# One-hots times the cutoff: made and stored in the one-head attention, loaded by the filter

## The chip, the cores and the metric

The kernel is one program on one core of a Trainium2 chip. A core has five engines, each with its own queue of instructions: TensorE (PE), VectorE (DVE), ScalarE (ACT), GpSimd (POOL), and SyncE (SP), which issues DMA transfers. Semaphores tie them together. The metric is the device time of one execution in microseconds (us), less is better.

## The reference

A graph network on 3125 nodes and 50000 edges: four layers, each with a residual and a layer norm. All of it is float32. Two parts matter here. The third attention of the second layer has one head of 128 channels; the filter of the third layer multiplies each edge's message by a filter and a cutoff, and sums the messages by destination:

```python
def _rgat(x, src, dst, etype, W, Q, K, b, heads, out_ch, n):      # third call: heads 1, out_ch 128
    ...
    alpha = _segment_softmax(alpha, dst, n)
    msg = (out_j.reshape(-1, heads, out_ch) * alpha[..., None]).reshape(-1, heads * out_ch)
    return jax.ops.segment_sum(msg, dst, num_segments=n) + b

h1 = h @ aw_W + aw_b                                              # the filter: _L2_gnn_ref
C = 0.5 * (jnp.cos(edge_weight * (PI / CUTOFF)) + 1.0)
Wf = ssp(ssp(edge_attr @ m1_W + m1_b) @ m2_W + m2_b)
Wf = Wf * C[:, None]
msg = h1[src] * Wf
agg = jax.ops.segment_sum(msg, dst, num_segments=n_nodes)
```

## The kernel before

The edges are sorted by destination and dealt into KS = 432 steps of P = 125 edges, each step belonging to one tile of 125 destination nodes. Both parts sum a step's messages by one product on PE: a one-hot matrix of 125 edges by 125 places in the tile (`sel`), times the 125 rows of messages. The one-hot is made by DVE: `iota` compared with `dloc`, the place of each edge's destination, for HF = 4 steps in one operation of 125x500. `cut` holds the cutoff of each edge.

**attention** runs three times: twice with four heads (H == 4) and last with one (H == 1, phase "sum3", the narrow attention). It goes by blocks of T = 12 steps, NS = 36 blocks, each in PARTS = 3 parts of four steps. POOL gathers the source rows of each step by an indirect DMA into `gx`, which holds three blocks; it waits only for the products that read the buffer three blocks back (`summed`). DVE scores the block after next as soon as its twelve gathers have landed (`score`), computes the softmax weights of the next block, and between these makes the one-hots of each part (`pick`, which counts `parted`) and adds PE's products to `agg` (`add_part`). ACT scales the gathered rows by the weights; PE does the products. SP loads one mask per block when `mask_used` says that a buffer is free. At the start of a block DVE's queue reads six numbers from memory into registers (`part_tiles`): which tile each part begins in, and whether a part spans two tiles, in which case its four steps are added one by one.

**filter_sum** goes by turns of four steps, 108 turns, in a loop of two (`q` is 0 or 1). POOL gathers the rows of `h2` into `gx`; SP loads the edges' attributes (`ea`). PE computes the hidden layer (`hidden`, L2390), the filter (`filters`, L2400) and the sums by destination (L2417). ACT computes the logarithms of softplus. The order is written out by hand, and several turns are in flight. In turn n DVE copies the cutoffs (`cl`, L2484), makes the one-hots (`sel`, L2485), finishes the filter `f2` once ACT's logarithm of turn n is there (L2489), multiplies filter, cutoff and gathered rows, one operation a step (`ms`, L2493), counts `ms_made` for PE and `used` for POOL, reads the tile numbers (`node_tiles`), finishes the hidden layer of turn n + 3 (`make_h1`, L2460), takes PE's filter product of turn n + 2 (`make_f2`, L2464), and adds PE's sums of turn n to `agg` (four operations, L2503).

Between the two lies nodes_mix, which works on nodes, not on edges.

## Time and profile before

| what | us |
|---|---|
| device time, median of 3 runs | 6739.39 (6736.36 to 6741.33) |
| profiled execution, device time | 6756.12 |
| its span | 6754.3 |
| granted TensorE clock over the span | 0.769 |
| one-head attention, gathers of POOL first to last issue | 3782.3 to 4440.3 |
| filter, loop of 108 turns | about 4694 to 5837 |

The profiled execution is 16.7 us above the median of the others, and 1.8 us of it lie outside the span. Times within the trace are us from the start of the span. "idle before <-releaser" is how long an engine stood still before an instruction and what ended it; "issue" is time in which its queue did work of its own (registers, branches, loads of numbers) and waited for nothing that the profile shows. DVEq and SPq are the queues of these engines.

### The profile page before, as it was taken

The numbers are of one execution on the slowest core, as the hardware profiler recorded it, in microseconds if no ns is written. First come the engines' busy times: TensorE is split into PE (matmuls) and PEld (weight loads), VectorE is DVE, ScalarE is ACT, GpSimd is POOL, SyncE is SP. The second block draws the span as 40 slices with busy tenths as digits, with TensorE's granted clock in tenths as the row PEclk, the third lists the DMA queues.
The fourth block names the chain that finished last, engine by engine and source line by source line (L and its number), as shares of the span: only waits on it lengthen the run. The fifth ranks groups of instructions, "written<-read, shape, count | busy, mean of one in ns | idle before, by whom it ended". The sixth has DMA issues, their size and how long they took to land. (4 is left out here: it accounts for less than half of the span.)

```text
span 6754.3 us, 80950 instructions
## 1 busy us (share of the span) xinstructions
PE 4441.0 (66%) x17924; PEld 3187.3 (47%) x17925; DVE 3214.4 (48%) x7726; ACT 2012.5 (30%) x4713; POOL 3593.5 (53%) x2941
## 2 busy tenths in 40 slices
PE   5699620885766778577677444467777777765553
PEld 5588610543555554455557333344545555443332
DVE  6566556213544522444443233343777777523334
ACT  0122200002655511455550122212555555410000
POOL 0244310467766647776647778721444444228885
PEclk9999855887887889787776555556999999876555
DMA  0000012225655523665532222222222222223333
GB/s 7 24 11 11 8 33 65 68 65 126 170 149 140 140 66 73 157 162 146 145 100 53 44 45 46 45 60 59 58 58 59 58 58 58 59 79 84 84 84 73
DMA packets 487821, 511.66 MB, mean 76 GB/s; under 512 B 307562, under 2 KB 372575, under 8 KB 487289
## 3 DMA queue, kind: packets, MB, share of 16 engines
q0 software_dynamic: 359872, 381.65, 23.6%
q1 hardware_dynamic: 127670, 127.35, 6.8%
q14 instruction: 233, 1.91, 0.1%
q8 instruction: 46, 0.75, 0.0%
HBM read 440.64 MB, written 65.22 MB: 75 GB/s over the span
## 5 line engine op out<-in xcount | busy, mean ns | idle before, releaser
L1198 POOL DMA_INDIRECT sum_gx_sb<-scratch_xw,keep_k_row_step_sb x1296 | 1599.8, 1234 | 564.1 <-issue 361.9
L1295 PE MATMUL sum_a_ps<-sum_gx_sb,sum_sel_sb 125*125 125x258 f32 (+1 forms) x4320 | 1241.6, 452 | 557.7 <-ACT sum_gx_sb L1231 234.9
L1295 PEld LDWEIGHTS sum_a_ps<-sum_gx_sb,sum_sel_sb 125*125 125x125 f32 x4320 | 955.9, 247 | 757.8 <-issue 563.2
L1231 ACT ACTIVATE sum_gx_sb<-sum_gx_sb,sum_wt_sb 125x129 f32<-125x129 f32 x3312 | 985.1, 398 | 492.5 <-DVE sum_wt_sb L1423 446.7
L2354 POOL DMA_INDIRECT filter_gx_sb<-scratch_h,keep_k_src_step_sb x432 | 520.6, 1205 | 678.0 <-DVEq L2495 531.7
L2782 POOL DMA_INDIRECT source_gx_sb<-scratch_h,source_grouped_sb x432 | 537.0, 1243 | 156.0 <-issue 118.9
L2794 PE MATMUL source_s_ps<-source_gx_sb,source_sel_sb 125*125 125x257 f32 x864 | 378.9, 615 | 313.6 <-DMA source_gx_sb<-scratch_h,source_grouped_sb 311.5
L1107 POOL DMA_INDIRECT scratch_grouped<-keep_k_value_sb,keep_k_place_sb x400 | 477.9, 1195 | 123.5 <-issue 123.5
L2400 PE MATMUL filter_ps<-filter_m_sb,filter_h_sb 128*125 128x256 f32 x1760 | 439.5, 406 | 39.9 <-DVE filter_f_sb L2464 39.9
L2794 PEld LDWEIGHTS source_s_ps<-source_gx_sb,source_sel_sb 125*125 125x125 f32 x864 | 252.5, 306 | 440.0 <-issue 196.3
L2400 PEld LDWEIGHTS filter_ps<-filter_m_sb,filter_h_sb 128*125 128x125 f32 x1760 | 343.9, 201 | 186.0 <-issue 132.7
L2417 PE MATMUL filter_ps<-filter_ms_sb,filter_sel_sb 125*125 125x256 f32 x864 | 243.2, 430 | 211.7 <-DVEq L2494 211.7
L2819 DVE TENSOR_TENSOR keep_agg_sb<-source_s_ps,keep_agg_sb 125x257 f32 x432 | 184.4, 427 | 395.4 <-PE source_s_ps L2794 384.3
L1443 DVE TENSOR_TENSOR keep_agg_sb<-sum_a_ps,keep_agg_sb 125x516 f32 (+1 forms) x360 | 202.3, 562 | 262.4 <-PE sum_a_ps L1295 143.0
L532 POOL TENSOR_TENSOR turn_lm_sb<-turn_lt_sb,turn_masks_sb 128x512 f32<-128x512 f32 x23 | 29.3, 1273 | 537.5 <-DVE turn_lt_sb L466 537.5
L1590 PE MATMUL attend_x_ps<-attend_w_sb,attend_ht_sb 128*125 128x512 f32 (+1 forms) x800 | 283.4, 528 | 37.3 <-ACT attend_ht_sb L2060 31.3
L2417 PEld LDWEIGHTS filter_ps<-filter_ms_sb,filter_sel_sb 125*125 125x125 f32 x864 | 170.2, 206 | 275.6 <-DVEq L2494 250.5
L2390 PE MATMUL filter_ps<-filter_ea_sb,filter_m_sb 51*128 51x500 f32 x444 | 239.8, 664 | 24.5 <-DMA filter_ea_sb<-in_ea_t 24.5
L2425 ACT ACTIVATE filter_lg_sb<-filter_f_sb 125x1024 f32<-125x1024 f32 x109 | 115.4, 1059 | 468.9 <-DVE filter_f_sb L2464 274.3
L2460 DVE SCALAR_TENSOR_TENSOR filter_h_sb<-filter_ps,filter_lg_sb 128x1000 f32<-128x1000 f32 x111 | 133.2, 1200 | 241.4 <-issue 202.2
L1430 DVE TENSOR_TENSOR sum_sel_sb<-sum_iota_sb,keep_k_dloc_sb 125x500 f32<-125x500 f32 x324 | 219.9, 679 | 50.7 <-issue 32.5
L2431 ACT ACTIVATE filter_lg_sb<-filter_lg_sb,filter_half_sb 128x1000 f32<-128x1000 f32 x220 | 238.8, 1132 | 7.6
(504 smaller groups left out, 7082.6 us busy)
## 6 DMA issues: line engine op xcount, KB each, us to landing
sum_gx_sb<-scratch_xw,keep_k_row_step_sb POOLq DMA_INDIRECT x1296
scratch_xw<-gate_xsb_sb SPq DMA_DIRECT2D x50, 253.9 KB
scratch_xw<-attend_xsb_sb SPq DMA_DIRECT2D x50, 253.9 KB
filter_ea_sb<-in_ea_t SPq DMA_DIRECT2D x444, 24.4 KB
filter_gx_sb<-scratch_h,keep_k_src_step_sb POOLq DMA_INDIRECT x432
source_gx_sb<-scratch_h,source_grouped_sb POOLq DMA_INDIRECT x432
sum_mk_sb<-scratch_masks SPq DMA_DIRECT2D x72, 93.9 KB
scratch_grouped<-keep_k_value_sb,keep_k_place_sb POOLq DMA_INDIRECT x400
```

The source lines that it names most:

```text
L1107: nc.gpsimd.indirect_dma_start(out=dr["grouped"], out_offset=bass.IndirectOffsetOnAxis(ap=keep["place"][:, t:t + 1], axis=0), in_=keep["va ...
L1198: nc.gpsimd.indirect_dma_start(out=gx[:, q, j, :], out_offset=None, in_=table, in_offset=bass.IndirectOffsetOnAxis(ap=keep["row_step"][:, ...
L1231: last = nc.scalar.activation(here, here, ACT.Copy, scale=wt[q][:, h, j:j + 1])
L1295: last = mm(psa[b][0:P, half, 0:BF], sel[:, 0, p, j, :], gx[:, q, at, half * BF:(half + 1) * BF], **flags)
L1590: mm(pr["psx"][r][0:P, 0:pr["width"]], x, pr["w"][:, b, r, :], start=(n == 0), stop=(n == len(blocks) - 1))
L2354: nc.gpsimd.indirect_dma_start(out=gx[:, q, j, :], out_offset=None, in_=dr["h2"], in_offset=bass.IndirectOffsetOnAxis(ap=keep["src_step"][ ...
L2390: last = mm(ps1[q][:, o, 0:C4], m1[0:51, 128 * o:128 * o + 128], ea[0:51, q].rearrange("p j e -> p (j e)"), start=True, stop=True)
L2400: last = mm(ps2[0:P, j, :], h1[q][:, b, j * P:j * P + P], m2[:, b, :], start=(b == 0), stop=(b == 1))
L2417: last = mm(ps3[0:P, j, :], sel[:, j, :], ms[:, j, :], start=True, stop=True)
L2431: nc.scalar.activation(lg[:], lg[:], ACT.Ln, scale=0.5, bias=half[0:lg.shape[0], :]).then_inc(made, 1)
L2782: nc.gpsimd.indirect_dma_start(out=gx[:, h % RING, j, :], out_offset=None, in_=dr["h3"], in_offset=bass.IndirectOffsetOnAxis(ap=grouped[:, ...
L2794: nc.tensor.matmul(pss[q % 2][0:P, j, 0:W], sel[:, q % 2, j, :], gx[:, q, j, :], start=True, stop=True).then_inc(summed, 1)
```

## The change

The one-hots of a step, times the cutoff of its edges, are made in the one-head attention, from the one-hots that `pick` has just made there: one 125x500 DVE operation a part (108 in all), into `cuts`. SP stores each (250 KB) to a scratch tensor `hots` in device memory. The filter loads them again, one transfer a turn, into `sel`, which is double now. So the filter makes no one-hots, copies no cutoffs, loads no `iota`, and `ms` is filter times gathered rows, one operation of 125x1024 a turn. SP's list is written anew: the loads of attributes are the same in number, each behind the same product of PE; behind each in the loop stands a wait for `summed` and the load of one-hots for two turns later.

```diff
@@ attention
+    cuts = mem.sb("cuts", [P, T // HF, HF, P]) if H == 1 else None
...
@@ attention, SP
             sp.dma_start(iota[:], dr["c_iota"][:, 0:128]).then_inc(landed, 16)
+            if H == 1:
+                for p in range(PARTS):
+                    sp.nop().then_inc(cut_out[p], 16)
...
+            def store_cuts(s):
+                for p in range(PARTS):
+                    sp.wait_ge(cut_made, s * PARTS + p + 1)
+                    sp.dma_start(dr["hots"][:, bass.ds((s * T + p * HF) * P, HF * P)], cuts[:, p].rearrange("p j n -> p (j n)")).then_inc(
+                        cut_out[p], 16)
+
             with sp.Fori(0, NS // 3 - 1) as i:
                 for q in range(3):
                     sp.wait_ge(mask_used, 3 * i + q + 1)
                     sp.dma_start(mk[:, q, :], dr["masks"][bass.ds(3 * i + q + 3, 1), 0:HT, :].rearrange(
                         "o p c -> p (o c)")).then_inc(m_in[q], 16)
+                    if H == 1:
+                        store_cuts(3 * i + q)
+            if H == 1:
+                for s in range(NS - 3, NS):
+                    store_cuts(s)
+                for p in range(PARTS):
+                    sp.wait_ge(cut_out[p], 16 * (NS + 1))
@@ attention, DVE, pick
                 dve.drain()
                 dve.nop().then_inc(parted, 1)
+                if H == 1:
+                    dve.wait_ge(cut_out[p], s * 16 + 16)
+                    vec.tensor_tensor(cuts[:, p], sel[:, 0, p],
+                                      keep["cut"][:, bass.ds(s * T + p * HF, HF)].unsqueeze(2).broadcast_to([P, HF, P]),
+                                      ALU.mult).then_inc(cut_made, 1)
@@ filter_sum
-    cl, sel = mem.sb("cl", [P, HF]), mem.sb("sel", [P, HF, P])
+    sel = mem.sb("sel", [P, 2, HF, P])
@@ filter_sum, SP
-            sp.dma_start(iota[:], dr["c_iota"]).then_inc(landed, 16)
...
+            def load_hots(n, q):
+                sp.dma_start(sel[:, q].rearrange("p j n -> p (j n)"), dr["hots"][:, bass.ds(n * (HF * P), HF * P)]).then_inc(
+                    hot_in[q], 16)
+
             sp.wait_ge(ea_free, 1)
-            load(0, 0)
-            load(HF, 1)
-            with sp.Fori(0, TURNS) as i:
+            for n in range(5):
+                if n >= 2:
+                    sp.wait_ge(hid, n - 1)
+                load(n * HF, n % 2)
+                if n < 2:
+                    load_hots(n, n)
+            with sp.Fori(0, TURNS - 1) as i:
                 for q in range(2):
-                    sp.wait_ge(hid, 2 * i + q + 1)
-                    load((i + 1) * U2 + q * HF, q)
-            sp.wait_ge(hid, 2 * TURNS + 1)
-            load(KS + U2, 0)
+                    sp.wait_ge(hid, 2 * i + q + 4)
+                    load(i * U2 + (q + 5) * HF, 1 - q)
+                    sp.wait_ge(summed, 2 * i + q + 1)
+                    load_hots(2 * i + q + 2, q)
@@ filter_sum, PE
                     pe.wait_ge(ms_made, n + 1)
                     pe.wait_ge(added, n + 1)
+                    pe.wait_ge(hot_in[q], i * 16 + 16)
                     for j in range(HF):
-                        last = mm(ps3[0:P, j, :], sel[:, j, :], ms[:, j, :], start=True, stop=True)
+                        last = mm(ps3[0:P, j, :], sel[:, q, j, :], ms[:, j, :], start=True, stop=True)
@@ filter_sum, DVE
-                    vec.tensor_copy(cl[:], keep["cut"][:, bass.ds(i * U2 + q * HF, HF)])
-                    vec.tensor_tensor(sel[:], iota[0:P, 0:P].unsqueeze(1).broadcast_to([P, HF, P]),
-                                      keep["dloc"][:, bass.ds(i * U2 + q * HF, HF)].unsqueeze(2).broadcast_to([P, HF, P]),
-                                      ALU.is_equal)
                     dve.wait_ge(log2_made, n + 1)
                     vec.scalar_tensor_tensor(f2[q][:], f2[q][:], 0.0, lg2[q][:], ALU.max, ALU.add)
                     dve.drain()
                     dve.wait_ge(x_in[q], (i + 1) * (16 * HF))
-                    for j in range(HF):
-                        vec.scalar_tensor_tensor(ms[:, j, :], f2[q][:, j, :], cl[:, j:j + 1], gx[:, q, j, :], ALU.mult, ALU.mult)
+                    vec.tensor_tensor(ms[:], f2[q][:], gx[:, q], ALU.mult)
                     dve.drain()
@@ build
+    dr["hots"] = nc.dram_tensor("scratch_hots", (P, KS * P), F32, kind="Internal").ap()
```

DVE in the filter's loop, second half (q = 1) of before, from the last addition of the turn before to the next hidden layer. "ISA", "REGISTER_ALU" and "TENSOR_LOAD" rows are work of the queue.

```order
L2503 TENSOR_TENSOR keep_agg_sb<-filter_ps,keep_agg_sb 125x256
L2484 ISA
L2484 COPY filter_cl_sb<-keep_k_cut_sb 125x4
L2485 REGISTER_ALU
L2485 TENSOR_TENSOR filter_sel_sb<-filter_iota_sb,keep_k_dloc_sb 125x500
L2489 SCALAR_TENSOR_TENSOR filter_f_sb<-filter_f_sb,filter_lg_sb 125x1024
L2493 SCALAR_TENSOR_TENSOR filter_ms_sb<-filter_f_sb,filter_cl_sb,filter_gx_sb 125x256 x4
L1121 REGISTER_ALU
L1121 TENSOR_LOAD keep_k_nk_sb
L1121 ISA x8
L2457 REGISTER_ALU
L2460 SCALAR_TENSOR_TENSOR filter_h_sb<-filter_ps,filter_lg_sb 128x1000
```

and of after:

```order
L2530 TENSOR_TENSOR keep_agg_sb<-filter_ps,keep_agg_sb 125x256
L2517 SCALAR_TENSOR_TENSOR filter_f_sb<-filter_f_sb,filter_lg_sb 125x1024
L2520 TENSOR_TENSOR filter_ms_sb<-filter_f_sb,filter_gx_sb 125x1024
L1121 ISA
L1121 TENSOR_LOAD keep_k_nk_sb
L1121 ISA x8
L2489 REGISTER_ALU
L2492 SCALAR_TENSOR_TENSOR filter_h_sb<-filter_ps,filter_lg_sb 128x1000
```

The copy, the one-hots and three of the four multiplications are gone; the finishing of the filter follows the addition directly.

DVE in the one-head attention, from the one-hots of a block's first part to the first addition of the next block, before:

```order
L1430 TENSOR_TENSOR sum_sel_sb<-sum_iota_sb,keep_k_dloc_sb 125x500
L1503 UNCONDITIONAL_BRANCH
L1503 ISA
L1131 TENSOR_LOAD keep_k_part_sb
L1131 ISA x12
...
L1430 TENSOR_TENSOR sum_sel_sb<-sum_iota_sb,keep_k_dloc_sb 125x500
L1458 COMPARE_AND_BRANCH
L1447 REGISTER_ALU
L1451 ISA
L1451 SCALAR_TENSOR_TENSOR keep_agg_sb<-keep_agg_sb,sum_fac_sb,sum_a_ps 125x129
```

and after:

```order
L1448 TENSOR_TENSOR sum_sel_sb<-sum_iota_sb,keep_k_dloc_sb 125x500
L1459 TENSOR_TENSOR sum_cuts_sb<-sum_sel_sb,keep_k_cut_sb 125x500
L1526 UNCONDITIONAL_BRANCH
L1526 ISA
L1131 TENSOR_LOAD keep_k_part_sb
...
L1448 TENSOR_TENSOR sum_sel_sb<-sum_iota_sb,keep_k_dloc_sb 125x500
L1458 ISA
L1459 REGISTER_ALU
L1459 TENSOR_TENSOR sum_cuts_sb<-sum_sel_sb,keep_k_cut_sb 125x500
L1481 COMPARE_AND_BRANCH
L1470 REGISTER_ALU
L1474 ISA
```

Each one-hot operation has a multiplication behind it: the first stands ahead of the load of the six numbers, the second ahead of the first addition, the third in the same way ahead of the second addition.

SP in the filter's loop, one half (q = 1) of after; before, the same list had no rows of L2394:

```order
L2391 ISA
L2391 TENSOR_LOAD keep_k_etile_sb
L2391 ISA x2
L2392 ISA
L2392 DMA filter_ea_sb<-in_ea_t 50x125
L2394 ISA
L2394 DMA filter_sel_sb<-scratch_hots 125x500
L2404 REGISTER_ALU
L2404 COMPARE_AND_BRANCH
```

The load of the one-hots stands behind the four loads of attributes.

## Rows read from the trace of the kernel before

**Rows 1.** Busy time by stretch: one-head attention early, late, its end, and the filter.

```profile
core 0: us, PE busy (x) PEld busy (x) DVE busy (x) ACT busy (x) POOL busy (x), PEclk, DMA share, GB/s
3782.00:4060.00 278.00, 108.39 (x483) 87.62 (x484) 94.44 (x345) 52.31 (x171) 222.23 (x183) 0.50 0.21 46
4060.00:4430.00 370.00, 160.84 (x734) 132.50 (x733) 144.83 (x527) 82.26 (x272) 296.23 (x243) 0.51 0.21 46
4684.00:5837.00 1153.00, 897.24 (x3047) 588.99 (x3045) 817.14 (x1409) 666.31 (x655) 511.00 (x425) 0.93 0.24 57
```

**Rows 2.** Who waited for whom in the filter: total us, times, longest.

```profile
DVE filter_h_sb L2460 <- issue: 202.2, 101, 2.1
DVE keep_agg_sb L2503 <- issue: 54.8, 324, 0.2
DVE filter_h_sb L2460 <- ACT filter_lg_sb L2431: 10.0, 5, 2.3
DVE filter_h_sb L2460 <- PE filter_ps L2400: 4.1, 2, 2.1
```

**Rows 3.** Timeline of DVE, one turn: start, us, operation, idle before.

```profile
5211.57 0.42 DVE L2503 TENSOR_TENSOR keep_agg_sb<-filter_ps,keep_agg_sb 125x256 f32 x1 [0.17 <-issue]
5212.20 0.17 DVE L2484 COPY filter_cl_sb<-keep_k_cut_sb 125x4 f32 x1 [0.20 <-issue]
5212.31 0.68 DVE L2485 TENSOR_TENSOR filter_sel_sb<-filter_iota_sb,keep_k_dloc_sb 125x500 f32<-125x500 f32 x1
5212.90 1.22 DVE L2489 SCALAR_TENSOR_TENSOR filter_f_sb<-filter_f_sb,filter_lg_sb 125x1024 f32<-125x1024 f32 x1
5214.21 1.67 DVE L2493 SCALAR_TENSOR_TENSOR filter_ms_sb<-filter_f_sb,filter_cl_sb,filter_gx_sb 125x256 f32<-125x256 f32 x4
5217.81 1.20 DVE L2460 SCALAR_TENSOR_TENSOR filter_h_sb<-filter_ps,filter_lg_sb 128x1000 f32<-128x1000 f32 x1 [1.93 <-issue]
5218.93 1.22 DVE L2464 TENSOR_TENSOR filter_f_sb<-filter_ps,filter_mb_sb 125x1024 f32<-125x1024 f32 x1
5220.06 0.41 DVE L2503 TENSOR_TENSOR keep_agg_sb<-filter_ps,keep_agg_sb 125x256 f32 x1
5228.69 1.20 DVE L2460 SCALAR_TENSOR_TENSOR filter_h_sb<-filter_ps,filter_lg_sb 128x1000 f32<-128x1000 f32 x1 [2.07 <-issue]
```

**Rows 4.** Timeline of PE, the same place, and its first turn.

```profile
5205.56 1.99 PE L2417 MATMUL filter_ps<-filter_ms_sb,filter_sel_sb 125*125 125x256 f32 x8 [1.59 <-DVEq L2494]
5207.48 1.94 PE L2390 MATMUL filter_ps<-filter_ea_sb,filter_m_sb 51*128 51x500 f32 x4
5210.03 3.69 PE L2400 MATMUL filter_ps<-filter_m_sb,filter_h_sb 128*125 128x256 f32 x16 [0.60 <-DVE filter_f_sb L2464]
5215.96 3.56 PE L2417 MATMUL filter_ps<-filter_ms_sb,filter_sel_sb 125*125 125x256 f32 x8 [2.25 <-DVEq L2494]
4668.78 3.67 PE L2390 MATMUL filter_ps<-filter_ea_sb,filter_m_sb 51*128 51x500 f32 x4 [22.22 <-DMA filter_ea_sb<-in_ea_t]
```

**Rows 5.** Timeline of ACT, one turn.

```profile
5209.97 1.06 ACT L2425 ACTIVATE filter_lg_sb<-filter_f_sb 125x1024 f32<-125x1024 f32 x1 [3.37 <-DVE filter_f_sb L2464]
5214.05 2.17 ACT L2431 ACTIVATE filter_lg_sb<-filter_lg_sb,filter_half_sb 128x1000 f32<-128x1000 f32 x2
```

**Rows 6.** One-head attention, by line: busy us, mean ns, idle before; then POOL's line alone, ns min/median/max.

```profile
L1198 POOL DMA_INDIRECT sum_gx_sb<-scratch_xw,keep_k_row_step_sb x432 | 527.8, 1222 | 131.7 <-issue 125.0 <-PE sum_a_ps L1295 6.7
L1430 DVE TENSOR_TENSOR sum_sel_sb<-sum_iota_sb,keep_k_dloc_sb 125x500 f32<-125x500 f32 x108 | 73.4, 680 | 21.4 <-issue 14.8 <-PE sum_a_ps L1295 3.2
L1198 POOL DMA_INDIRECT sum_gx_sb<-scratch_xw,keep_k_row_step_sb x432: 1197/1203/1710, 3782.3 to 4440.3; - x144
```

**Rows 7.** A long gather on POOL, and the one-hots on DVE beside it.

```profile
3977.61 1.67 POOL L1198 DMA_INDIRECT sum_gx_sb<-scratch_xw,keep_k_row_step_sb  x1 [0.30 <-issue]
3977.53 0.68 DVE L1430 TENSOR_TENSOR sum_sel_sb<-sum_iota_sb,keep_k_dloc_sb 125x500 f32<-125x500 f32 x1
3978.59 0.29 DVE L1443 TENSOR_TENSOR keep_agg_sb<-sum_a_ps,keep_agg_sb 125x129 f32 x1 [0.38 <-issue]
```

**Rows 8.** Idle time of DVE before its scoring, 4060 to 4430; before its scan, 3782 to 4477.

```profile
  DMA sum_gx_sb<-scratch_xw,keep_k_row_step_sb: 29.2, 13
DVE sum_both_sb L1382 <- issue: 142.9, 35, 7.0
```

**Rows 9.** A stretch with nothing but transfers of 125 rows on the DMA engines.

```profile
4485.00:4490.00 5.00, 4.97 (x9) 2.36 (x10) 0.00 (x0) 0.00 (x0) 0.00 (x0) 0.50 0.33 111
```

**Rows 10.** End of the one-head attention on DVE, and what stands behind it.

```profile
4471.56 0.68 DVE L1430 TENSOR_TENSOR sum_sel_sb<-sum_iota_sb,keep_k_dloc_sb 125x500 f32<-125x500 f32 x1 [0.30 <-issue]
4474.81 0.29 DVE L1443 TENSOR_TENSOR keep_agg_sb<-sum_a_ps,keep_agg_sb 125x129 f32 x1 [1.42 <-PE sum_a_ps L1295]
4476.35 0.16 DVE L2263 MEMSET mix_ones_sb<- 1x125 f32 x1 [1.25 <-PEq L87]
```

More of the change, by code:

```diff
@@ L1178, in attention @@
         "landed", "held", "first_in", "edge_in", "spread", "q_summed", "q_taken", "blank", "cleared"))
+    cut_made, cut_out = nm("cut_made"), [nm(f"cut_out{p}") for p in range(T // HF)]
     x_in, m_in = [nm(f"x{q}") for q in range(3)], [nm(f"m{q}") for q in range(3)]
@@ L2331, in filter_sum @@
     m1, m2, mb = mem.sb("m1", [64, D]), mem.sb("m2", [128, 2, D]), mem.sb("mb", [P, D])
-    iota, half = mem.sb("iota", [128, 512]), mem.sb("half", [128, 1])
+    half = mem.sb("half", [128, 1])
     lg1, h1 = ([mem.sb(f"{n}{q}", [128, 2, C4]) for q in range(2)] for n in ("lg1", "h1"))
@@ L2341, in filter_sum @@
          "f2_made", "log2_made", "ms_made", "summed", "added"))
-    x_in, e_in = [mem.sem(f"x{q}") for q in range(2)], [mem.sem(f"e{q}") for q in range(2)]
+    x_in, e_in, hot_in = ([mem.sem(f"{n}{q}") for q in range(2)] for n in ("x", "e", "hot"))
     vec, mm = nc.vector, nc.tensor.matmul
@@ L2348, in _ @@
         def _(pool):
-            pool.wait_ge(landed, 16 * 5)
+            pool.wait_ge(landed, 16 * 4)
             for step in range(KS):
@@ L2401, in filters @@
                 last.then_inc(filt, 1)
-            pe.wait_ge(landed, 16 * 5)
+            pe.wait_ge(landed, 16 * 4)
             hidden(0, 0, 16 * HF)
@@ L2474, in _ @@
                 dve.nop().then_inc(sem, 1)
-            dve.wait_ge(landed, 16 * 5)
+            dve.wait_ge(landed, 16 * 4)
             make_h1(0, 0)
```

1 line of the change is left out of this document (added).

## The prediction

> **What bounds the kernel now.** The kernel is a row of phases with nothing running across their borders, so the change is worth the sum of what it does to the one-head attention and to the filter. I read the busy times by stretch first, then who waits for whom, then the timeline of the engine that waits for nobody.
>
> The filter takes 1153 us [rows 1]. No engine looks full: PE 897, DVE 817, ACT 666. The waits tell more. DVE waits for another engine only 14 us in all, in the first turns; the rest of its idle time is "issue" [rows 2]: the tile numbers being read (202 us, 2.0 a turn), and the register work between additions. Busy or issuing, DVE is full. PE waits for its `ms` (1.59 and 2.25 us) and for `make_f2` (0.60) [rows 4], ACT for DVE too [rows 5]. A turn lasts 10.26 us in one half of the loop and 10.88 in the other (hidden layer at 5217.81 to the next at 5228.69; one turn back it stood 10.26 earlier) [rows 3]: 10.57 on the mean. So the filter is bound by DVE.
>
> The one-head attention is bound by POOL. 432 gathers of 1.22 us and 0.30 of issue between them follow each other from 3782.3 to 4440.3, 1.52 a step, 18.3 a block, and POOL waits for the products only 6.7 us in all [rows 6]. DVE is a third busy (145 of 370 us) [rows 1], but much of the rest is issue: it waits for landed gathers only 29.2 us in the 370 us from 4060 to 4430 [rows 8], 20 blocks, 1.45 us a block. That is its slack, not the two thirds.
>
> **The change, part by part.**
>
> 1. Filter, copy and one-hots gone. They sit between 5212.20 and the start of the next operation at 5212.90 [rows 3]: 0.70 us. The 0.20 of issue ahead of the copy stays, since the drain and the count of the last addition do. The wait for the logarithm needs a register that was worked out under the one-hots; I take 0.03 off for it.
>
> 2. Filter, four multiplications become one. The four take 1.67 us. The new one is a 125x1024 product of two operands; the same size takes 1.22 on this engine, with one input in PSUM (L2464) or two in SBUF (L2489) [rows 3]. Gain 0.45.
>
> 3. Together 0.70 + 0.45 - 0.03 = 1.12 us a turn, 108 turns: 121 us. Bounds: with the 0.20 of issue going too, 1.35 a turn, 146 us; with 0.2 of register work uncovered, 0.95, 103 us. I take the value from the timeline itself.
>
> 4. What is late next in the filter. The turn would be 10.57 - 1.12 = 9.45 us. PE needs 1.99 + 1.94 + 3.69 = 7.62 [rows 4], or 9.2 when its sums take 3.56. ACT's ring: from its start at 5209.97 to the end of the first logarithm at 5215.2 (5214.05 plus half of 2.17), then `make_h1` and `make_f2` (2.25 from start to end of both, starts 1.12 apart, 1.22), then ACT again: 5.2 + 2.4 = about 7.7 [rows 3, 5]. The longest ring spans two turns: `ms`, PE's sums (2.0) and hidden (1.94), ACT to its first logarithm (5.2), then on DVE `make_h1`, `make_f2`, four additions, `f2` and `ms`, about 7.5: 16.7 in two turns, 8.4 each. All lie below 9.45, so DVE stays the bound and the whole 121 us counts. POOL needs 4 x 1.5 = 6.0.
>
> 5. Filter, loads of one-hots. A transfer of 125 rows goes at 111 GB/s, with a third of the DMA engines' time in use [rows 9]; 250 KB (256 thousand bytes) take 2.3 us. Each is issued when the sums of turn n are done and is needed at those of turn n + 2, some 17 us later. Hidden. The DMA share of 0.24 [rows 1] becomes about 0.35. In SP's queue the loads of attributes keep their triggers; behind the wait for `summed` stands only the next turn's load, which waits for a later product of PE. At the start two one-hot loads stand between the first three loads of attributes: +1 us (0 to 3). The load of `iota` that goes hid under DVE's clearing of `agg`: nothing.
>
> 6. Attention, 108 multiplications on DVE. Like the one-hots they are 125x500, 0.68 each [rows 6]. The one of a block's first part is issued ahead of the reading of six numbers, 4 us of issue a block (142.9 in 35) [rows 8], and hides under it. The other two stand ahead of an addition that now waits 0.38 for issue [rows 7]; that work would run under the multiplication, so each adds about 0.2 + 0.6 - 0.38 = 0.45. So 0.9 us a block against a slack of 1.45: no cost. Upper bound: nothing overlaps, 3 x 0.85 = 2.55, 1.1 beyond the slack over 20 blocks, 22 us, less what POOL tolerates once: when DVE scores, it has two parts of the block behind it and POOL needs only the first one's buffer, an estimated 5 us: 17 us. Before 4060 the waits are longer.
>
> 7. Attention, POOL slowed. Most gathers take 1203 ns, some up to 1710 [rows 6]. The long ones start while DVE makes one-hots: 1.67 us at 3977.61, when the one-hots ran from 3977.53 to 3978.21 [rows 7]. In all the gathers take 527.8 - 432 x 1.203 = 8.1 us more than their median, beside 108 one-hot operations. The multiplications are another 108 of the same size with both inputs in SBUF, and POOL is the bound there: +8 us (0 to 16). The Trainium skill gives the reason (SBUF — State Buffer, "Who interferes with whom"): a DVE instruction with two SBUF inputs contends with a GpSimd instruction that reads SBUF. The trace agrees. The same section says that a probe showed `tensor_tensor` not stalling descriptor generation; by that the term would be 0 and the time 8 us less.
>
> 8. Attention, the stores. One of 2.3 us on a third of the DMA engines per 6.1 us of POOL, beside gathers that use a share of 0.21 [rows 1, 9]. No engine comes near full. DVE's wait for the store of a block ago is long over. At the end of the phase the last multiplication ends at about 4473, its store must land (issue 0.3, transfer 2.3, landing some 1 to 2 more), about 4477, where the last addition ended at 4475.1 [rows 10]; with the delay of the second multiplication +2.5 us (1 to 5). The Trainium skill (DMA: Bandwidth & Descriptors, "Why a DMA increments its semaphore by 16 and not by 1") says why it is a third: a transfer from SP uses the largest number up to 16 that divides its rows, for 125 that is 5.
>
> Sum: -121 + 1 + 8 + 2.5 = -109.5 us. On the profiled execution: span 6754.3 to 6644.8. It lies 16.7 us above the median of the timed runs; I let this difference stand: 6739.4 - 109.5 = 6630.
>
> **The rivals.**
>
> A. DVE's slack in the attention is used up. For it: 1.45 us a block is little, and the branch and register work may not overlap. Against: the six numbers hide a third of it. The upper bound of part 6: +17, 6647.
>
> B. The filter runs into PE at its lower clock. Sums behind an idle time of 2.25 us took 3.56, behind 1.59 only 1.99; the hidden product behind a long wait took 3.67 for 1.94 [rows 4]. The granted clock is 0.93 of 2.4 GHz in the filter and 0.50, the level of 1.2 GHz, in the attention [rows 1]. If in every other turn both were slow, that turn would be 3.56 + 3.67 + 3.69 = 10.9, the mean 10.2, and the gain 0.4 x 108 = 43: 6739.4 - 43 + 11.5 = 6708. Against: PE would idle less, about 0.4 and 1.1 us a turn, and at 1.59 it was not slow.
>
> C. Slower than before: the stores govern the attention. The three stores a block are a closed chain with DVE (`cut_out`) and with the landing of gathers on the same DMA engines. Up to 6.1 us a part they are hidden. Each us beyond costs 108. From 6.1 + 109.5/108 = 7.1 us a store (36 GB/s, a third of the measured 111) the change loses; at 9 us it would be +313 - 109.5 = +204, 6943. For it: rows of 2000 bytes at a pitch of 216000, beside gathers. Against: 3 times the measured time would be needed.
>
> D. More gain than I count: the issue ahead of the copy goes with it and POOL isn't slowed: -146 + 3.5, 6597.
>
> **How the numbers follow.** Forecast 6630: 0.72. A 6647: 0.14. B 6708: 0.06. C: 0.03. D 6597: 0.05. The forecast's own bounds are 6739.4 - 146 + 1 = 6594 and 6739.4 - 103 + 3 + 16 + 5 = 6660; few of the terms will stand at the same end, so the range is 6602 to 6660, which leaves out B, C, the half of D and little else. A measurement of this kernel can tell about 0.2% (13 us) from no change. Faster by more than that: 0.96, all but C and a sliver; same 0.01; slower 0.03.
>
> **What would show it.** In the profile after, the filter's turns should be 9.1 and 9.8 us, with idle time of DVE before `make_h1` still "issue"; "ACT" or "PE" there would speak for the rings of part 4 or for B. The new `ms` should take 1.22 us and the sums 2.0 in both halves. In the attention the gathers' mean should rise from 1222 to about 1240 ns, with their wait for PE still near 6.7 us; a wait of 20 us or more there is A. Stores well over 6 us, or DVE waiting before the multiplication, is C. The prediction is wrong if DVE isn't what sets the filter's turn at 9.45.

## The result, and the profile after

The changed kernel takes 6621.23 us, median of 4 runs (6613.47 to 6625.9), beside 6740.18 (6736.36 to 6741.33) of the kernel before: a ratio of 0.9823, 95% interval 0.9806 to 0.984, 119 us less. The forecast was 6630, 109.5 less. The profiled execution of after took 6613.47 us, its span 6611.7.

By phase, from the timelines (first gather of the one-head attention to the first instruction of the phase behind it, and the same for the filter):

| us | before | after | difference | forecast |
|---|---|---|---|---|
| one-head attention | 694.0 | 712.3 | +18.3 | +10.5 |
| filter | 1183.0 | 1042.2 | -140.8 | -120 |
| both | 1877.0 | 1754.5 | -122.5 | -109.5 |

The spans of the two profiled executions differ by 142.6 us. 18.8 us of that lie ahead of everything that the change touches: in the profiled execution of before the first gather came at 3782.3, in that of after at 3763.5, and in the later profiles of before's variants it ranged over 3764 to 3786.

Busy time of after by stretch: one-head attention early and late, and the filter. It answers to [rows 1].

```profile
core 0: us, PE busy (x) PEld busy (x) DVE busy (x) ACT busy (x) POOL busy (x), PEclk, DMA share, GB/s
3764.00:4042.00 278.00, 105.03 (x465) 84.42 (x465) 114.73 (x371) 52.20 (x171) 223.13 (x181) 0.50 0.32 78
4042.00:4412.00 370.00, 157.69 (x715) 129.96 (x716) 179.67 (x576) 78.65 (x260) 296.18 (x237) 0.51 0.34 85
4653.00:5695.00 1042.00, 832.87 (x3068) 551.15 (x3068) 702.44 (x874) 672.47 (x661) 519.48 (x432) 0.99 0.35 91
```

The filter's DMA share is the 0.35 that was expected; the attention's went from 0.21 to 0.32 and 0.34. DVE has 115 us less in the filter and 35 us more in 370 us of the attention, PE's granted clock in the filter went from 0.93 to 0.99.

Who waited for whom in the filter of after, as in [rows 2]: total us, times, longest.

```profile
DVE filter_h_sb L2492 <- issue: 209.5, 107, 2.0
DVE keep_agg_sb L2530 <- issue: 54.4, 324, 0.2
DVE filter_h_sb L2492 <- ACT filter_lg_sb L2463: 28.3, 4, 15.0
DVE filter_f_sb L2517 <- issue: 25.8, 53, 0.5
```

DVE still waits for nobody but itself: 107 of its waits before `make_h1` are issue, and the four for ACT all lie ahead of 4699, in the first turns. It is still the bound. Timeline of DVE in after, the two halves of the loop, as [rows 3]:

```profile
5193.12 0.42 DVE L2530 TENSOR_TENSOR keep_agg_sb<-filter_ps,keep_agg_sb 125x256 f32 x1 [0.17 <-issue]
5194.03 1.23 DVE L2517 SCALAR_TENSOR_TENSOR filter_f_sb<-filter_f_sb,filter_lg_sb 125x1024 f32<-125x1024 f32 x1 [0.49 <-issue]
5195.42 1.23 DVE L2520 TENSOR_TENSOR filter_ms_sb<-filter_f_sb,filter_gx_sb 125x1024 f32<-125x1024 f32 x1 [0.16 <-issue]
5198.62 1.20 DVE L2492 SCALAR_TENSOR_TENSOR filter_h_sb<-filter_ps,filter_lg_sb 128x1000 f32<-128x1000 f32 x1 [1.97 <-issue]
...
5202.64 0.43 DVE L2530 TENSOR_TENSOR keep_agg_sb<-filter_ps,keep_agg_sb 125x256 f32 x1 [0.17 <-issue]
5203.18 1.22 DVE L2517 SCALAR_TENSOR_TENSOR filter_f_sb<-filter_f_sb,filter_lg_sb 125x1024 f32<-125x1024 f32 x1
5204.47 1.23 DVE L2520 TENSOR_TENSOR filter_ms_sb<-filter_f_sb,filter_gx_sb 125x1024 f32<-125x1024 f32 x1
5207.65 1.20 DVE L2492 SCALAR_TENSOR_TENSOR filter_h_sb<-filter_ps,filter_lg_sb 128x1000 f32<-128x1000 f32 x1 [1.95 <-issue]
```

A turn takes 9.03 us (5198.62 to 5207.65) and in the other half 9.51, where it was 10.26 and 10.88. From the end of the last addition to the finishing of `f2` it is 0.11 us now (5203.07 to 5203.18); in [rows 3] it was 0.91 (5211.99 to 5212.90). From the start of `ms` to the next hidden layer it is 3.18, where it was 3.60.

PE in after, as [rows 4]: the sums take 1.99 us in both halves, behind 1.00 and 1.53 us of idle time.

```profile
5187.24 1.99 PE L2449 MATMUL filter_ps<-filter_ms_sb,filter_sel_sb 125*125 125x256 f32 x8 [1.00 <-DVEq L2521]
5196.81 1.99 PE L2449 MATMUL filter_ps<-filter_ms_sb,filter_sel_sb 125*125 125x256 f32 x8 [1.53 <-DVEq L2521]
```

The gathers of the one-head attention in after (busy us, mean ns, idle before), as [rows 6], which has 527.8, 1222 and 6.7:

```profile
L1200 POOL DMA_INDIRECT sum_gx_sb<-scratch_xw,keep_k_row_step_sb x432 | 539.2, 1248 | 133.3 <-issue 125.9 <-PE sum_a_ps L1313 7.4
```

DVE's wait for landed gathers in 370 us of after, 4041 to 4411, as [rows 8], which has 29.2 in 13:

```profile
DVE sum_sc_sb L1392 <- DMA sum_gx_sb<-scratch_xw,keep_k_row_step_sb: 12.3, 8, 5.0
```

First to last gather takes 671.0 us (+13.0, of which 11.4 are longer gathers), and the tail from the last gather to the next phase 41.3 (+5.3). In the tail SP issues the last store at 4470.53, and DVE's last addition ends at 4472.54, but the next phase starts only at 4475.92, behind the landing of that store. SP's wait for it, total us, times, longest:

```profile
SPq L1236 <- DMA scratch_hots<-sum_cuts_sb: 3.8, 1, 3.8
```

### The profile page after: what moved, and what is told of

The parts are those of the page before. It is cut to its first block and busy times, and to the rows that moved or that the text cites. A ratio compares the mean times of both kernels' runs of the same rounds, so it can differ in the third digit from the quotient of the medians.

```text
span 6611.7 us, 81270 instructions
## 1 busy us (share of the span) xinstructions
PE 4356.9 (66%) x17924; PEld 3140.3 (47%) x17925; DVE 3158.4 (48%) x7294; ACT 2007.4 (30%) x4713; POOL 3596.5 (54%) x2941
## 5 line engine op out<-in xcount | busy, mean ns | idle before, releaser
L2431 PE MATMUL filter_ps<-filter_m_sb,filter_h_sb 128*125 128x256 f32 x1760 | 407.1, 385 | 50.7 <-DVE filter_f_sb L2496 50.7
L2431 PEld LDWEIGHTS filter_ps<-filter_m_sb,filter_h_sb 128*125 128x125 f32 x1760 | 322.4, 188 | 180.5 <-issue 135.6
L532 POOL TENSOR_TENSOR turn_lm_sb<-turn_lt_sb,turn_masks_sb 128x512 f32<-128x512 f32 x23 | 29.2, 1272 | 536.5 <-DVE turn_lt_sb L466 536.5
L2449 PE MATMUL filter_ps<-filter_ms_sb,filter_sel_sb 125*125 125x256 f32 x864 | 214.8, 392 | 135.3 <-DVEq L2521 135.3
L1242 ACT ACTIVATE sum_wexp_sb<-sum_dw_sb 48x126 f32<-48x126 f32 (+1 forms) x108 | 33.3, 308 | 719.2 <-DVEq L1431 719.2
L2449 PEld LDWEIGHTS filter_ps<-filter_ms_sb,filter_sel_sb 125*125 125x125 f32 x864 | 153.4, 187 | 196.4 <-issue 102.5
L2421 PE MATMUL filter_ps<-filter_ea_sb,filter_m_sb 51*128 51x500 f32 x444 | 219.0, 614 | 24.8 <-DMA filter_ea_sb<-in_ea_t 24.8
```

The lines of the kernel that those rows point to most:

```text
L2431: last = mm(ps2[0:P, j, :], h1[q][:, b, j * P:j * P + P], m2[:, b, :], start=(b == 0), stop=(b == 1))
L2449: last = mm(ps3[0:P, j, :], sel[:, q, j, :], ms[:, j, :], start=True, stop=True)
```

## The experiments

Two things were to be settled: whether the filter's gain and the attention's loss come from the parts of the change that the prediction put them down to, and why both were larger than forecast. "Attention" is always from the first gather to the next phase, and the unchanged attention took 694.0, 693.3, 693.4, 693.0 and 693.4 us in five profiles. The attention of after is also in two other kernels, those of experiment 8 and of after with idle instructions (experiment 9): it took 712.3, 711.1 and 709.8 us. So what is told below against after's 712.3 may be up to 2.5 us less.

| kernel | us, median | ratio to before, 95% | attention | filter | turns |
|---|---|---|---|---|---|
| before | | | 694.0 | 1183.0 | 10.26 / 10.88 |
| after | 6621.23 | 0.9823 (0.9806 to 0.984) | 712.3 | 1042.2 | 9.03 / 9.51 |
| multiplications alone | 6736.89 | 0.9993 (0.9984 to 1.0003) | 703.0 | 1169.9 | 10.26 / 10.66 |
| stores alone | 6742.72 | 1.0004 (0.9995 to 1.0014) | 710.2 | 1170.0 | 10.26 / 10.64 |
| one product alone | 6700.81 | 0.9927 (0.9911 to 0.9944) | 693.3 | 1137.1 | 9.80 / 10.42 |
| after, multiplied by ACT | 6618.95 | 0.9819 (0.9802 to 0.9835) | 704.5 | 1049.2 | 9.03 / 9.61 |
| after, stored twice | 6693.3, one run | | 773.9 | 1042.1 | 9.02 / 9.51 |
| after, 128 rows | 6632.3 | 0.9818 (0.9801 to 0.9835) | 705.5 | 1041.8 | 9.02 / 9.51 |
| after, 128 rows and ACT | 6625.38 | 0.9812 (0.9799 to 0.9825) | 696.8 | 1055.4 | 9.02 / 9.74 |
| after, no finishing of `f2` | 6499.61, one run | | 711.1 | 911.5 | 7.82 / 8.23 |

Rows of different batches have their own runs of before beside them (6741.13, 6754.96 and 6747.22 us), so the ratios compare, the medians only roughly.

**1. The multiplications alone.** The kernel before, with the multiplications of the attention and nothing else:

```diff
@@ before, attention, DVE, pick
                 dve.nop().then_inc(parted, 1)
+                if H == 1:
+                    vec.tensor_tensor(cuts[:, p], sel[:, 0, p],
+                                      keep["cut"][:, bass.ds(s * T + p * HF, HF)].unsqueeze(2).broadcast_to([P, HF, P]),
+                                      ALU.mult)
```

> The filter is that of before; the one-head attention makes the one-hots times the cutoff on DVE (108 multiplications of 125x500), and nothing is stored or loaded. Theory DVE (the multiplications lengthen the gathers, because both of their inputs are in SBUF): the gathers' mean in that phase rises from 1222 to about 1248 ns as in the changed kernel, first to last issue 658 to about 670 us, total +10 to +14. Theory DMA (it is the stores that lengthen the gathers): mean stays at 1222, total within 3 us of before.

The attention took 9.0 us longer. POOL's gathers in this kernel:

```profile
L1200 POOL DMA_INDIRECT sum_gx_sb<-scratch_xw,keep_k_row_step_sb x432 | 535.9, 1241 | 131.7 <-issue 124.7 <-PE sum_a_ps L1303 7.0
```

They are 8.1 us longer in all than in [rows 6], and POOL's wait for PE, 7.0, stays what it was. So the multiplications on DVE slow the gathers by 8 us, and their own time on DVE costs nothing. The total of +10 to +14 us didn't come all the same: the whole kernel took as long as before, since its filter, whose code is that of before, took 13.1 us less, in the half with the jump (experiment 9).

Is it any work of DVE that slows a gather, or work with two inputs in SBUF? The filter of before has the answer. In its loop the gathers run beside `make_h1`, `make_f2` and the additions, each of which has one input in PSUM, and not beside the one-hots, the finishing of `f2` or `ms`, which have both inputs in SBUF. They take 1205 ns in the mean, where those of the attention take 1222:

```profile
L2354 POOL DMA_INDIRECT filter_gx_sb<-scratch_h,keep_k_src_step_sb x432 | 520.6, 1205 | 678.0 <-DVEq L2495 531.7
```

So 1.2 us of DVE with one input in PSUM leave the gathers at their usual length, while 0.68 us with both inputs in SBUF don't [rows 7].

**2. The stores alone.** The attention of after with the multiplication left out: SP stores a tile of zeros 108 times, and the filter is that of before.

```diff
@@ after, attention, DVE, pick
                     dve.wait_ge(cut_out[p], s * 16 + 16)
-                    vec.tensor_tensor(cuts[:, p], sel[:, 0, p],
-                                      ...
-                                      ALU.mult).then_inc(cut_made, 1)
+                    dve.nop().then_inc(cut_made, 1)
```

> The filter is that of before; the one-head attention stores 108 times 250 KB of a blank tile at the places of the changed kernel, and multiplies nothing. Theory DVE: gathers' mean 1222, first to last issue 658, and only the landing of the last store at the end of the phase: total +3 to +5. Theory DMA: mean about 1248, total +15.

Neither theory has this: the attention took 16.2 us longer, and not by longer gathers:

```profile
L1200 POOL DMA_INDIRECT sum_gx_sb<-scratch_xw,keep_k_row_step_sb x432 | 526.1, 1218 | 141.7 <-issue 123.8 <-PE sum_a_ps L1313 18.0
```

POOL waits 11.3 us more for the products, of which shorter gathers and less issue give 3 back, and the tail is 43.9 us (36.0 before). The whole kernel isn't longer than before beyond the noise, since its filter took 13.0 us less, as in experiment 1. A store in the tail, in two stretches of 2 us of the same trace:

```profile
4452.00:4454.00 2.00, 0.00 (x0) 0.00 (x0) 0.00 (x0) 0.00 (x0) 0.00 (x0) 0.50 0.32 102
4454.00:4456.00 2.00, 0.80 (x2) 0.50 (x2) 1.18 (x4) 0.00 (x0) 0.00 (x0) 0.50 0.21 75
```

102 GB/s at a share of 0.32, five of sixteen. Together with experiment 1 this would give +25 in after; it has +18.3. So the two don't add: with the multiplications in place the stores cost 9.3 us (712.3 less 703.0; 6.8 by the shortest of the three attentions of after), still more than the forecast's 2.5. About 2.1 of it is the landing at the end: from the last addition's end to the next phase after has 3.4 us, experiment 1 has 1.3.

Another number moved. DVE's queue loads six numbers a block from SBUF (the `member` columns and tiles, L1131). Durations in ns, min/median/max, in before:

```profile
L1131 DVEq TENSOR_LOAD <-keep_k_part_sb x36: 804/1158/1493, 3823.3 to 4466.8; - x36
```

with the stores alone:

```profile
L1131 DVEq TENSOR_LOAD <-keep_k_part_sb x36: 821/1310/3567, 3805.0 to 4460.8; - x36
```

and in after:

```profile
L1131 DVEq TENSOR_LOAD <-keep_k_part_sb x36: 811/1418/2034, 3804.4 to 4463.9; - x36
```

All 36 take 40.8 us in before, 41.1 with the multiplications alone, 45.8 in after and 65.5 with the stores alone. The order in DVE's queue fits this: in after the load starts beside the multiplication and so ahead of the store of its result, with the stores alone it starts just behind the count that releases the store. That this is why the two costs don't add was not tested.

**3. One product alone.** The filter of before with the single 125x1024 product; the cutoff is left out of the computation.

```diff
@@ before, filter_sum, DVE
-                    for j in range(HF):
-                        vec.scalar_tensor_tensor(ms[:, j, :], f2[q][:, j, :], cl[:, j:j + 1], gx[:, q, j, :], ALU.mult, ALU.mult)
+                    vec.tensor_tensor(ms[:], f2[q][:], gx[:, q], ALU.mult)
```

> The kernel before with one product of 125x1024 (filter times gathered rows) in place of four with the cutoff; the cutoff is left out of the result, its copy and the one-hots are still made. If the gain of a turn is worked out rightly: 0.45 us of 1.30 a turn come from here, turns 9.8 and 10.4 us, total -48 (0.45 x 108). If fewer instructions also free the queue: 0.6 a turn, -65.

```profile
5206.50 1.22 DVE L2489 SCALAR_TENSOR_TENSOR filter_f_sb<-filter_f_sb,filter_lg_sb 125x1024 f32<-125x1024 f32 x1
5207.88 1.23 DVE L2492 TENSOR_TENSOR filter_ms_sb<-filter_f_sb,filter_gx_sb 125x1024 f32<-125x1024 f32 x1 [0.16 <-issue]
```

That is DVE's timeline here: 1.23 us where four operations took 1.67. The turns are shorter by 0.46 in both halves, the filter by 45.9 us, 0.43 a turn. The rest of after's gain, 95 us or 0.88 a turn, comes with the one-hots and the copy, or, for some 0.07, with the half that has the jump (experiment 9); the forecast had 0.67 for it.

**4. The multiplications on ACT.** After, with `cuts` made by four activations a part (`Copy` with the cutoff as scale) instead of DVE's operation. DVE now waits before the next one-hots of a part until ACT has read the last.

```diff
@@ after, attention, ACT
+                for j in range(HF):
+                    last = nc.scalar.activation(cuts[:, p, j], sel[:, 0, p, j], ACT.Copy,
+                                                scale=cs_all[:, bass.ds(s * T + p * HF + j, 1)])
+                last.then_inc(cut_made, 1)
```

> The changed kernel with the one-hots times the cutoff made by ScalarE (four activations of 125x125 a part, the cutoff as the scale) in place of DVE. ScalarE stands idle 159 us in that phase waiting for weights. Theory DVE: the gathers' mean falls back from 1248 to about 1222, first to last issue 671 to 659, total 9 to 13 us below the changed kernel. Theory DMA: mean stays at 1248, total within 3 us of the changed kernel. A rival for both: the softmax weights of the next block stand behind the third part's activations on ScalarE and DVE waits for them; then DVE's wait before L1436 of the changed kernel grows from 0.4 us in all to 30 or more, and the phase isn't shorter.

```profile
L1200 POOL DMA_INDIRECT sum_gx_sb<-scratch_xw,keep_k_row_step_sb x432 | 527.8, 1222 | 133.7 <-issue 124.4 <-PE sum_a_ps L1331 9.3
```

The gathers are at the 1222 ns of before, although the same data are multiplied and stored: it is DVE's operation that lengthens them. The attention is 7.8 us shorter than in after. The rival's sign stayed away: DVE's wait for ACT before L1436 of after is 0.4 us here too. But the filter is 7.0 us longer, 5.4 of it in one half of the loop (9.61 for 9.51), and that took most of the gain back: the 9 to 13 us for the whole kernel didn't come.

**5. Each part stored twice**, to two tensors, 216 stores in all; DVE's and SP's waits count both.

```diff
@@ after, attention, SP, store_cuts
-                    sp.dma_start(dr["hots"][...], cuts[:, p]...).then_inc(cut_out[p], 16)
+                    for name in ("hots", "hots2"):
+                        sp.dma_start(dr[name][...], cuts[:, p]...).then_inc(cut_out[p], 16)
```

> The changed kernel, each part of the one-hots stored twice, to two tensors. By the prediction's 2.3 us a store, two take 4.6, under the 6.1 us of a part: the attention (first gather to the start of the next phase, 712 us) grows by the landing alone, to about 720. By the 4.3 us that a lone store seems to take in the run with stores only, two take 8.6 and govern: 108 x 8.6 = 930 us, and POOL waits some 200 us.

Neither number came: the attention took 773.9 us, 61.6 more than in after. POOL's gathers, and DVE's loads of numbers:

```profile
L1200 POOL DMA_INDIRECT sum_gx_sb<-scratch_xw,keep_k_row_step_sb x432 | 533.7, 1235 | 189.2 <-issue 120.4 <-PE sum_a_ps L1314 68.8
```

```profile
L1131 DVEq TENSOR_LOAD <-keep_k_part_sb x33: 820/2653/6386, 3819.3 to 4470.5; - x33
```

POOL now waits 68.8 us for the products, and a load of six numbers (33 of the 36 are in this view) takes 2.65 us in the median. All 36 together take 95.0 us, 54 more than in before. Another 21 us stand behind the jump of the attention's outer loop, taken eleven times: DVE's queue has 2.9 us there in the median in before, 2.8 in after and 5.9 here. What the stores' queue takes in after is in the view of DMA queues over the attention (packets, MB, share of 16 engines); in before it was 0.6%:

```profile
q1 hardware_dynamic: 14832, 27.80, 13.3%
```

12.7% of 16 engines over 712 us are 1447 us of one engine, 13.4 a store, 2.7 us on five engines. Two of them would be 5.4 us in a part of 6.1 (an estimate; in this run it was 2.5 a store, by 22.2% over 774 us). So they don't stay hidden until they fill a part: their cost grows well before.

**6. 128 rows.** The theory by now: a store of 125 rows uses five of the sixteen engines for 2.7 us, and whatever of the gathers goes through these waits. The landing of the gathers speaks for it: from the start of a gather to its landing it is 3.4 us in the median with the multiplications alone (not the 2.3 of the expectation below), 3.8 in after. Stored and loaded with 128 rows (three of zeros), the same bytes can go over all sixteen.

```diff
-    cuts = mem.sb("cuts", [P, T // HF, HF, P]) if H == 1 else None
+    cuts = mem.sb("cuts", [128, T // HF, HF, P]) if H == 1 else None
...
-    sel = mem.sb("sel", [P, 2, HF, P])
+    sel = mem.sb("sel", [128, 2, HF, P])
...
-    dr["hots"] = nc.dram_tensor("scratch_hots", (P, KS * P), F32, kind="Internal").ap()
+    dr["hots"] = nc.dram_tensor("scratch_hots", (128, KS * P), F32, kind="Internal").ap()
```

> The changed kernel with stores and loads of 128 rows in place of 125 (three rows of zeros that nobody uses), which can be dealt to all 16 DMA engines. If the stores harm because they lie on five engines: in the attention the gathers land 2.3 us after their issue again (3.8 in the changed kernel), and first gather to next phase falls from 712 to about 703, the cost of the multiplications alone (703.0 in e1_mults). If it is the bytes: 712. The filter stays at 9.03 and about 9.5 us. Total 0 to 9 us below the changed kernel.

A store in the tail of this kernel, by us:

```profile
4470.00:4471.00 1.00, 0.93 (x4) 0.96 (x5) 0.58 (x1) 1.00 (x5) 0.00 (x0) 0.50 0.00 0
4471.00:4472.00 1.00, 1.00 (x6) 0.82 (x4) 0.00 (x0) 1.00 (x5) 0.00 (x0) 0.50 0.56 206
4472.00:4473.00 1.00, 0.13 (x1) 0.00 (x0) 0.00 (x0) 0.55 (x2) 0.00 (x0) 0.50 0.14 50
```

256 KB in two stretches of 1 us, 206 GB/s at a share of 0.56 in the first: more than five engines. DVE's loads of numbers are back at before's duration,

```profile
L1131 DVEq TENSOR_LOAD <-keep_k_part_sb x36: 807/1152/1584, 3815.5 to 4469.9; - x36
```

SP waits 1.6 us for the last store, where it waited 3.8,

```profile
SPq L1236 <- DMA scratch_hots<-sum_cuts_sb: 1.6, 1, 1.6
```

and the attention takes 705.5 us, 2.5 more than with the multiplications alone: the spread of a store over more engines is worth 6.8 us of the 9.3 (4.3 of 6.8 by the shortest attention of after). The filter, which loads the same rows, didn't change (1041.8), so its loads were hidden in either form.

**7. 128 rows and ACT together.** The edits of 4 and 6.

> The changed kernel with two edits together: the multiplications of the one-hots by the cutoff are made by ScalarE, four activations a part, and the parts are stored and loaded with 128 rows (three of them zeros). Theory: each edit takes away one of the two things that slow the gathers of the narrow attention, so that first gather to mix comes to 693 to 698 us (712.3 in the changed kernel, 704.5 with ScalarE alone, some 705.5 with 128 rows alone), with gathers of 1220 to 1224 ns in the mean and a tail behind the last gather of some 38 us; the filter's turns stay at 9.03 and 9.5 to 9.6 us. Sum: 6621 less 14 to 19, plus 5 if the jump half has 9.6: 6602 to 6612. Rival: both edits take away the same thing (contention at the queues), and together they give no more than one: 703 to 706 us, 6612 to 6619.

```profile
L1200 POOL DMA_INDIRECT sum_gx_sb<-scratch_xw,keep_k_row_step_sb x432 | 527.2, 1220 | 131.7 <-issue 122.5 <-PE sum_a_ps L1331 9.1
```

The attention takes 696.8 us, within 4 us of one that stores nothing, and 15.5 less than after: 6.8 and 7.8 alone, so the two losses are separate and add. It is also 7.7 and 8.7 less than with either edit alone, which doesn't hang on after's 712.3. The rival, one common cause, is out. But the whole kernel isn't clearly faster than after, and the 6602 to 6612 us didn't come: the filter takes 13.2 us more, 12.4 of it in the half with the jump (9.74, where 9.5 to 9.6 was expected).

```profile
5212.03 1.23 DVE L2534 SCALAR_TENSOR_TENSOR filter_f_sb<-filter_f_sb,filter_lg_sb 125x1024 f32<-125x1024 f32 x1 [0.71 <-issue]
```

The issue ahead of the finishing of `f2` is 0.71 us there, 0.49 in after, and DVE's code in the loop is the same.

**8. DVE's loop without the finishing of `f2`**, to see what is late next. The `relu` part of the second softplus is left out.

```diff
@@ after, filter_sum, DVE
-                    vec.scalar_tensor_tensor(f2[q][:], f2[q][:], 0.0, lg2[q][:], ALU.max, ALU.add)
-                    dve.drain()
                     dve.wait_ge(x_in[q], (i + 1) * (16 * HF))
-                    vec.tensor_tensor(ms[:], f2[q][:], gx[:, q], ALU.mult)
+                    vec.tensor_tensor(ms[:], lg2[q][:], gx[:, q], ALU.mult)
```

> The changed kernel without the operation that finishes the filter on DVE (L2517, 1.23 us): ms is the logarithm alone times the gathered rows, the relu part of the softplus is left out. DVE's own work falls from 9.27 to about 7.95 us a turn. By part 4 of the prediction the ring over two turns then stands at 8.4 - 0.65 = 7.8 and ACT's at 7.7: the turn becomes about 7.95, the filter phase falls by 108 x 1.3 = 140 us, and DVE begins to wait for ACT. If a ring was underrated: a turn of 8.5 or more, 80 us or less.

The turn fell from 9.27 to 8.03 us in the mean, 1.24 for an operation of 1.23. Who waited for whom, 4700 to 5500:

```profile
DVE filter_h_sb L2492 <- ACT filter_lg_sb L2463: 112.1, 54, 5.9
DVE filter_h_sb L2492 <- issue: 91.4, 46, 2.8
```

Half of the waits are put down to ACT's logarithm now, but they cost next to nothing: 2.08 us each in the mean, where those put down to issue have 1.99. The logarithm lands while DVE's queue reads the tile numbers. So the rings of ACT and PE fit into 8.03 us, and at 9.27 DVE alone is the bound; how much shorter than 8.03 they are isn't shown.

**9. The half with the jump.** One half of the filter's loop took 10.88 us in before but 10.66 and 10.64 in experiments 1 and 2, whose filter is that of before. Idle instructions on DVE ahead of the loop (8, 24 and 100 in before, 24 in after) give the loop's code another place in the program:

```diff
             make_f2(1, 1)
+            for _ in range(24):
+                dve.nop()
             with dve.Fori(0, TURNS) as i:
```

> The kernel before with eight empty instructions on DVE's queue ahead of the filter's loop and nothing else. In two kernels with the filter's code of before, but other code ahead of it, the half of the loop with the jump took 10.66 and 10.64 us where before took 10.88. If the place of the loop in the program sets this: that half changes here too, to something between 10.6 and 11.2, the other half stays 10.26. If something else in those kernels did it (the contents of the attention): 10.88 and 10.26 as before.

> The kernel before with 24 instructions that do nothing on VectorE, once, ahead of the filter's loop; nothing else differs. Theory: the half of the loop that has the jump costs more or less by where the loop's instructions lie in memory; then this shift moves the 10.87 us of that half to another value (10.64 to 10.90), while the other half stays at 10.26. Rival: the position has no part in it (8 such instructions changed nothing), and both stay.

> As the run with 24 idle instructions ahead of the filter's loop, with 100. Theory of the position: another value again in the half with the jump, 10.60 to 10.90. Rival: 10.87 as before, and the difference to the runs with 10.64 and 10.66 stays open.

> The changed kernel with 24 idle instructions on VectorE ahead of the filter's loop. Theory of the position: the half with the jump, 9.51 us, moves by up to 0.25 us either way (9.61 in the version with ScalarE's multiplications, whose code ahead of the loop is shorter on VectorE), the other stays at 9.03. Rival: 9.51 stays.

None of the four moved a turn by more than 0.01 us (10.26 / 10.87 three times, 9.02 / 9.51). Their times, one run each, were 6756.69, 6751.06, 6749.18 and 6621.89 us, all within 4 us of the unshifted kernels beside them (6754.96 and 6747.22 for the first three, 6621.23 for the last). With 24 idle instructions the copy of the jump half still stands behind 0.60 us:

```profile
5214.81 0.17 DVE L2486 COPY filter_cl_sb<-keep_k_cut_sb 125x4 f32 x1 [0.60 <-issue]
```

and with the stores alone behind 0.49, whose next hidden layer stands behind 1.95 where before's stands behind 2.07 [rows 3]:

```profile
5214.17 0.17 DVE L2507 COPY filter_cl_sb<-keep_k_cut_sb 125x4 f32 x1 [0.49 <-issue]
5219.88 1.20 DVE L2483 SCALAR_TENSOR_TENSOR filter_h_sb<-filter_ps,filter_lg_sb 128x1000 f32<-128x1000 f32 x1 [1.95 <-issue]
```

The theory of the position, as tried, falls. What sets the 0.49, 0.60 or 0.71 stays open: it is fixed within a program, differs between programs with the same loop, and is worth up to 0.23 x 54 = 12 us here.

## Why the prediction was right, point by point

**The bound.** DVE bounds the filter before and after, POOL the attention: right, by the waits of after, and by experiment 8, where 1.23 us less on DVE made the turn 1.24 shorter.

**Parts 1 to 3, the filter's gain.** The mechanism was right, the size was off: 1.12 us a turn was forecast, 1.23 and 1.37 came, 1.30 in the mean. The product's 0.45 came as 0.42 to 0.46. The mis-sized term is the issue ahead of the copy: "The 0.20 of issue ahead of the copy stays". 0.11 stayed, so copy and one-hots were worth 0.80 in the half without the jump, and the 0.03 for the register of the wait wasn't charged. The other 0.14 stands in the half with the jump, nearly all of it between the start of `ms` and the next hidden layer: 3.75 us became 3.20, 0.55 less where the other half has 0.42, and 0.10 of that is issue (2.07 to 1.97). Experiments 1 and 2 show that this half can lose 0.22 with no change to the filter at all, so it is no gain of this change that another kernel could count on. Without it the filter would have gained 1.23 x 108 = 133.

**Part 4, what is late next.** That all rings lie below 9.45 was right: in experiment 8 they fit into 8.03. Their sizes, 7.7 for ACT, 7.62 for PE and 8.4 for the one over two turns (7.8 without the finishing of `f2`), agree with that, but no run shows them. (From the start of `make_h1` to the end of `make_f2` the rows give 2.34, not 2.25; nothing hangs on it.)

**Part 5, the loads.** Hidden, as said: PE waited for none of them in after, and with more engines per load nothing changed. Of the +1 at the start 0.5 came: the first hidden product stands 15.8 us into the phase, in before 15.3. (125 rows of 2000 bytes are 250 thousand bytes, not 256; at 111 GB/s that is the same 2.3 us.)

**Part 6, the multiplications on DVE.** Right: 0.9 us a block of 1.45 was forecast, DVE's wait for gathers fell from 29.2 to 12.3 us over 20 blocks, 0.85 a block. POOL's wait for PE rose by 0.3 in experiment 1.

**Part 7, POOL slowed.** Right: +8 forecast, +8.1 in experiment 1, gone in experiment 4, 1248 ns in the mean in after for 1240. Of the two sentences of the Trainium skill (SBUF — State Buffer, "Who interferes with whom") the rule on a DVE instruction with two SBUF inputs is the one that the traces agree with: 108 such `tensor_tensor` operations added 8.1 us to the gathers, the same work on ACT none, and DVE's operations with one input in PSUM none. The other sentence, on a probe in which `tensor_tensor` didn't stall descriptor generation, would have made the term 0; the measurement decides against it for these gathers. By which port the gathers are held up, no run shows.

**Part 8, the stores.** This term was mis-sized: +2.5 forecast, +9.3 in after beyond the multiplications (6.8 by the shortest attention of after). Its own sum, the landing of the last store, was about right: 2.1 us. What it put at nothing is the rest, 4.7 to 7.2 us while the phase runs. "No engine comes near full" reads a mean over sixteen engines, but a store keeps five of them busy for 2.7 us of every 6.1. The part already had the reason for the five, by the Trainium skill (DMA: Bandwidth & Descriptors, "Why a DMA increments its semaphore by 16 and not by 1"), and used it for the duration alone. By the same rule 128 rows go over all sixteen; experiment 6 agrees, with a share of 0.56 where five engines give 0.31, and with it the cost falls to 2.5 us. What the stores of 125 rows lengthen is the time to the landing of gathers (3.4 to 3.8 us) and, as seen and not foreseen, the loads of numbers of DVE's queue; how the 9.3 divides between them isn't shown.

**The rivals.** A and B didn't come: POOL's wait for PE is 7.4 us, and the sums take 1.99 in both halves at a clock of 0.99. C didn't come, but its threshold was wrong: "Up to 6.1 us a part they are hidden" is refuted by experiment 5, where some 5 us a part cost 61.6 more than one store. D was half right, in that the filter's gain was near its upper bound (140.8 of 146), and half wrong, since POOL was slowed.

**The sum.** Two errors of opposite sign, 20.8 us too little gained in the filter and 7.8 too little lost in the attention, left 13 us between forecast and result by the phases of the profiles, 8.8 by the medians. That the second took more than a third of the first away is luck. The range holds the result, but the bounds of part 8 (1 to 5) didn't hold their term.

## What to carry to other kernels

When an engine's queue is the bound, count for a removed operation also the issue around it, and look at both halves of an unrolled loop. A DMA that is "hidden" by its mean share is priced by the engines that it occupies: move tiles of 125 rows as 128 before trusting such a sum. And a product that DVE makes from two inputs in SBUF beside GpSimd's gathers is charged to the gathers; ACT made the same product at no cost to them.

## What the runs showed of the hardware that was not expected

- A queue's load of six numbers from SBUF (1158 ns in the median) is lengthened by stores of 125 rows from SBUF: 1418 ns in after, 2653 (up to 6386) with two stores a part, and 1152 again when the same bytes went in 128 rows. It is work of DVE's queue, so it shows as "issue".
- With stores of 125 rows twice a part, the jump of the attention's outer loop on DVE's queue took 5.9 us in the median, 2.9 in before.
- DVE's 1.2 us operations with one input in PSUM left the gathers beside them at 1205 ns in the mean; those with both inputs in SBUF lengthened single gathers up to 1.7 us.
- A store of 250 KB in 125 rows went at 102 GB/s, one of 256 KB in 128 rows at 206 GB/s over one us.
- The issue time around the jump of the same loop was 0.49, 0.59, 0.60 or 0.71 us from program to program, and 100 idle instructions ahead of the loop didn't move it. Its cause is open.
